# One output projection of batch 1 behind the fourth expert, in place of two parts behind the third and the fourth

## The chip, the cores and the metric

The kernel runs on one core of a Trainium2 chip. The metric is the time of one execution on the device in microseconds (us), lower is better. The engines are named as in the profile: PE (TensorE, the matrix engine), PEld (its weight loads), DVE (VectorE), ACT (ScalarE), POOL (GpSimd) and SP (SyncE, which only issues DMAs here).

## The reference, cut to what matters

Two batches of 512 tokens of width 128 first attend to themselves and to 154 context rows with 16 heads of width 64, and then pass a mixture of eight experts of which each token uses two.

```python
x = x + _L0_xattn_ref(ctx_1024, _layernorm(x), ...)
    # softmax(q k^T / 8) v for 16 heads, out = concat(heads) @ Wout
x = x + _L0_ffn_ref(_layernorm(x), ...)
    # probs = softmax(x @ Wg); the two best of 8, scaled to sum 1
    # out = sum over experts of score * (relu(xm @ W1 + b1) @ W2 + b2)
```

In the kernel the 512 tokens of a batch give the queries, and tokens and context rows together (666) the keys and values.

## The kernel before

The program of each engine is written out by hand, in the order in which it runs; semaphores tie the engines together. An engine that waits holds up everything behind it in its own list.

**Attention.** A step `s` (0 to 15, `STEPS` = 16) handles one pair of heads of one batch; there are `PAIRS` = 8 pairs. `batch_of(s)` and `pair_of(s)` say which: steps 12 to 15 are the pairs 4 to 7 of batch 1. A step makes scores in the PSUM tensor `sc`, ACT takes the exponent, PE multiplies with the values, and ACT copies the unscaled output to `o_t[:, batch, pair, :]` (semaphore `o_copied`). The row sums go from PE through ACT (`copy_sum`, semaphore `sum_copied`) to DVE, which takes four reciprocals of them (L1052, `recip_done`). POOL then multiplies the output by them: `normalise(s)`, L1384, one 128x512 product, which raises `o_norm` by one. `o_norm` at 14 therefore says that pairs 4 and 5 of batch 1 are scaled too, at 16 that pairs 6 and 7 are.

**Output projection.** `out_project(b, bank, pairs)` multiplies, for each of four token tiles of 128 and each pair given, a 128x128 block of `o_t` by a 128x128 block of Wout (L592), and adds all of them up in one PSUM bank. For all eight pairs that is 32 products in the program; the trace has two matmuls for each, 64. For batch 1 the bank is `o_ps`, a half of `xo`. The last matmul of pair 7 raises `out_proj`, on which DVE waits in `x1_and_moments` (L1132).

**Experts.** The loop over `g` (0 to 15) takes eight experts of batch 0 and then eight of batch 1. `layer_one(g)` is six matmuls of 128x512 (L404 to L406, twice), ACT makes relu and a rounded copy of it (L919, L932, L947), POOL and DVE the remainder (`relu_lo`, L1355, L1361, L1190), and `layer_two(g - LAG)` with `LAG` = 2 is six matmuls again (L712, L713, L720). DVE weights an expert's output by the score and adds it up (`add_expert`, L1209 and L1215).

**What hangs on batch 1's projection.** DVE adds the residual (L1132) and takes moments; POOL takes the power (L1412); DVE normalises (L997); PE turns the result (`turn_x2(1)`, L649, behind `layer_one(6)`); DVE splits it; PE makes the gate's logits (L657, behind g = 7); DVE works out the scores; PE turns them (`turn_scores(1)`, L664, behind `layer_one(10)`); ACT copies them (L951); SP writes them to memory and reads them back in eight broadcasts (`spread`, L392). The last three experts scale their hidden values by these (`scale_hidden`, L1201).

**POOL around the change.** In its loop over `g`, POOL works on the remainder of the first half for every `g` (L1355), and between those: for g = 0 `normalise(12)`, `normalise(13)` and a remainder of W2 (L1348); for g = 1 `normalise(14)` and one of W2; for g = 2 two of W2, `normalise(15)`, and three more of W2.

Of the kernel before, what the change touches and what calls it, by code (L numbers as in the profile page):

```python
# [26 lines left out]
PAIRS = H // 2  # L27
STEPS = PAIRS * B
# [57 lines left out]
def xattn_moe(nc, x, ctx_in, g_m, b_m, g_l, b_l, wq, wkv, wout, wg, w1, b1, w2, b2, out):  # L86
    with ExitStack() as stack:
# [6 lines left out]
        def sem(name):  # L94
            return stack.enter_context(nc.semaphore(name))
# [76 lines left out]
        x1_ps = [mx[:, 0, :], o_ps]  # L172
# [78 lines left out]
        o_norm = sem("o_norm")  # L251
# [150 lines left out]
        def _(pe):  # L402
# [104 lines left out]
            def total(s):  # L507
                bank = sum_ps(s)
                if s < HALVED:
                    pe.wait_ge(acc_lo_done, s + 1)  # L510
                    for part in (acc_hi, acc_lo):
                        for h in range(2):
                            mm = pe.matmul(bank[h * HD:(h + 1) * HD, :], ones_h[0:KP, :], part[0:KP, h, :],  # L513
                                           start=(part is acc_hi), stop=(part is acc_lo))
                    mm.then_inc(sum_ready, 1)
                    return
                pe.wait_ge(added, (KT - 1) * (s + 1))
                for h in range(2):
                    mm = pe.matmul(bank[h * HD:(h + 1) * HD, :], ones[0:KP, :], psum_acc[0:KP, s % 2, h, :],
                                   start=True, stop=True)  # L520
                mm.then_inc(sum_ready, 1)
# [67 lines left out]
            def out_project(b, bank, pairs):  # L589
                for t in range(QT):  # L590
                    for r in pairs:
                        mm = pe.matmul(bank[:, t * P:(t + 1) * P], o_t[:, b, r, t * P:(t + 1) * P],  # L592
                                       wout_sb[:, r, :], start=(t == 0 and r == 0),
                                       stop=(t == QT - 1 and r == PAIRS - 1))
                if r == PAIRS - 1:
                    mm.then_inc(out_proj, 1)
# [49 lines left out]
            def turn_x2(b):  # L646
                pe.wait_ge(normed_ready, NORMED0 + QT * (b + 1))
                for t in range(QT):
                    mm = pe.transpose(x2_ps[b][:, t * P:(t + 1) * P], normed[:, b, t, :], ident[:, :])  # L649
                mm.then_inc(x2_turned, 1)  # L650

            def logits(b):
                pe.wait_ge(x2_copied, b + 1)
                if b:
                    pe.wait_ge(x1_ready, 2)
                for t in range(QT):
                    mm = pe.matmul(logits_ps[b][:, t * E:(t + 1) * E], kv_t[:, b, t * P:(t + 1) * P], wg_sb[:, :],  # L657
                                   start=True, stop=True)
                mm.then_inc(logits_ready, 1)

            def turn_scores(b):
                pe.wait_ge(score_ready, b + 1)
                for t in range(QT):
                    mm = pe.transpose(score_ps[b][0:E, t * P:(t + 1) * P], score[:, b, t, :], ident[:, :])  # L664
                mm.then_inc(score_turned, 1)

            def bias_term(b):
                pe.wait_ge(score_copied, b + 1)
                if not b:
                    pe.wait_ge(sum_copied, STEPS - 1)  # L670
                pe.matmul(bias_ps[b], b2_sb[:, :], score_t[:, b, :], start=True, stop=True).then_inc(bias_ready, 1)

            def layer_one(g):
                b, e = g // E, g % E
                if e == 0:
                    pe.wait_ge(x2_lo, b + 1)
                pe.wait_ge(w1_split, min(g + 1, E))
                for c in range(HC):
                    n = g * HC + c
                    if n < 2:  # L680
                        pe.wait_ge(exp_done, STEPS * KT - 1)
                    elif n < 4:
                        pe.wait_ge(sum_copied, STEPS - 1)
                        pe.wait_ge(o_copied, STEPS)
                    elif c == 0:
                        pe.wait_ge(r0_done, g - 1)
                    elif g - 2 in ON_POOL:
                        pe.wait_ge(r1_done, g - 1)
                    else:
                        second_low(pe, g - 2)  # L690
                    three(hid(n), w1_hi[:, e, c * P:(c + 1) * P], w1_lo[:, e, c * P:(c + 1) * P],
                          kv_hi[:, b, 0:N], kv_lo[:, b, 0:N]).then_inc(hid_ready, 1)

            def layer_two(g):
                e = g % E
                if g >= SCALED:
                    if g == SCALED:
                        pe.wait_ge(acc_v, SCALED - 1)
                elif g >= 3:
                    pe.wait_ge(acc_v, g - 2)  # L700
                elif g == 2:
                    pe.wait_ge(bias_copied, 1)
                elif g == 1:
                    pe.wait_ge(score_copied, 1)
                pe.wait_ge(w2_split, min(g + 1, E))
                first, last = g <= SCALED, g < SCALED or g == B * E - 1
                for half, at in enumerate(halves if g >= SCALED else [slice(0, N)]):
                    y = y_ps(g, half)[:, at]
                    for c in range(HC):
                        n = (g * HC + c) % FR  # L710
                        pe.wait_ge(hi1_done if c else hi0_done, g + 1)
                        pe.matmul(y, w2_hi(e)[:, c, :], relu_hi[:, n, at], start=(first and c == 0), stop=False)  # L712
                        pe.matmul(y, w2_lo(e)[:, c, :], relu_hi[:, n, at], start=False, stop=False)  # L713
                    for c in range(HC):
                        n = (g * HC + c) % FR
                        if c:
                            second_low(pe, g)
                        else:
                            pe.wait_ge(lo0_done, g + 1)
                        mm = pe.matmul(y, w2_hi(e)[:, c, :], relu_lo[:, n, at], start=False,  # L720
                                       stop=(last and c == HC - 1))
                    if last:
                        mm.then_inc(y_ready, 1)

            def turn_acc(b):
                pe.wait_ge(acc_v, SCALED if b else E)
                if b:
                    pe.wait_ge(out_ready, 1)
                else:
                    pe.wait_ge(bias_copied, 2)  # L730
                for t in range(QT):
                    mm = pe.transpose(o_ps[:, t * P:(t + 1) * P], acc_t(b)[:, t * P:(t + 1) * P], ident[:, :])
                mm.then_inc(acc_turned, 1)
# [19 lines left out]
            for g in range(B * E):  # L753
                layer_one(g)
                if g == 0:
                    turn_scores(0)
                if g == 1:
                    pe.wait_ge(exp_done, STEPS * KT)
                    total(s)
                if g == 2:  # L760
                    bias_term(0)
                if g == 6:
                    turn_x2(1)
                if g == 10:
                    turn_scores(1)
                if g == 11:
                    bias_term(1)
                if g >= LAG:
                    layer_two(g - LAG)
                if g == 2:  # L770
                    pe.wait_ge(sum_copied, STEPS)
                    pe.wait_ge(o_norm, STEPS - 2)
                    out_project(1, x1_ps[1], range(PAIRS - 2))
                if g == 3:
                    pe.wait_ge(o_norm, STEPS)
                    out_project(1, x1_ps[1], range(PAIRS - 2, PAIRS))
                if g == 7:
                    logits(1)
                if g == 12:
                    turn_acc(0)  # L780
# [681 lines left out]
```

## Time and profile before

| | |
|---|---|
| median of 3 runs | 339.58 us (339.53 to 339.75) |
| the profiled execution | 339.86 us |
| its span, from the first to the last instruction | 338.1 us |
| PE busy | 330.7 us, 98% of the span |
| POOL busy | 293.2 us, 87% |
| DVE busy | 276.4 us, 82% |
| ACT busy | 216.7 us, 64% |
| TensorE clock granted | 1.00 of full speed in all 40 slices |

The profiled execution is the one that the trace shows, and its time lies 1.76 us above its span. It is 0.28 us above the median of the three timed runs. Times in the rows are microseconds from the start of the span. The matmuls are pipelined, so that one listed with 0.39 us may follow the one before it after 0.23 us; the chain of work counts each with what it adds.

### The profile page before, as it was taken

What the parts mean: (1) busy time and instruction counts of PE and PEld (TensorE: products, weight loads), DVE (VectorE), ACT (ScalarE), POOL (GpSimd) and SP (SyncE); (2) the same over time, 40 slices, a digit from 0 to 9 for tenths busy, and PEclk for the clock granted to TensorE, in tenths of its full rate; (3) what the DMA queues carried; (4) which work ended last, traced back from release to release, by engine and by line L of the source; (5) the groups of instructions that cost most, each with busy time, mean ns of one, the idle gap of its engine ahead of it and who ended that gap; (6) DMA issues with size and microseconds to landing.
All of it is one profiled execution on the core that took longest, in us unless ns stands there. A gap on an engine that the chain in (4) does not pass through costs nothing.

```text
span 338.1 us, 6020 instructions
## 1 busy us (share of the span) xinstructions
PE 330.7 (98%) x2209; PEld 220.9 (65%) x2209; DVE 276.4 (82%) x413; ACT 216.7 (64%) x307; POOL 293.2 (87%) x190
## 2 busy tenths in 40 slices
PE   7899999999999999999999999999999999999986
PEld 6676666575747475666657574747585648888766
DVE  5989566988889899999998887989785879489475
ACT  2565678584949484766758585959553746587954
POOL 4549999999999999999999999999996599688763
PEclk9999999999999999999999999999999999999999
DMA  4640000000010100000000000000000006100531
GB/s 128 186 128 0 2 0 4 0 17 0 2 31 3 30 2 0 3 0 3 16 2 16 2 16 17 0 2 0 3 0 3 0 2 211 39 2 0 164 119 34
DMA packets 9050, 10.03 MB, mean 30 GB/s; under 512 B 1015, under 2 KB 6061, under 8 KB 9021
## 3 DMA queue, kind: packets, MB, share of 16 engines
q1 hardware_dynamic: 8725, 9.52, 9.0%
q8 instruction: 18, 0.29, 0.4%
q10 hardware_dynamic: 296, 0.13, 0.1%
q14 instruction: 11, 0.09, 0.1%
HBM read 9.09 MB, written 0.56 MB: 29 GB/s over the span
## 4 chain that ended last, share of the span: by engine, by line
PE 90%; DMA 3%; DVE 3%; ACT 1%; issue 1%; SPq 1%; POOL 0%; DVEq 0%
PE xo L503 23%; PE sc L483 21%; PE sc L489 6%; PE sc L404 5%; PE sc L405 4%; PE sc L406 4%; PE mx L435 3%; PE xo L435 3%; PE mx L592 2%; PE xo L592 2%; PE xo L513 2%; DMA spread<-score_rows 2%; PE sc L503 2%; PE mx L405 1%; PE mx L404 1%; PE mx L406 1%
## 5 line engine op out<-in xcount | busy, mean ns | idle before, releaser
L1377 POOL TENSOR_TENSOR psum_acc<-psum_acc,probs 111x1024 f32<-111x1024 f32 x64 | 164.9, 2576 | 7.0
L816 ACT ACTIVATE probs<-sc 111x1024 f32<-111x1024 f32 x94 | 96.2, 1027 | 17.8 <-PE sc L489 10.5
L483 PE MATMUL sc<-q_pair,k_pair 64*111 64x512 f32 x564 | 83.9, 401 | 0.4 <-ACT v_sb L806 0.4
L503 PE MATMUL xo<-probs,v_sb 111*64 111x512 f32 x360 | 82.7, 596 | 0.0
L483 PEld LDWEIGHTS sc<-q_pair,k_pair 64*111 64x111 f32 x564 | 43.7, 171 | 27.0 <-issue 11.5
L1052 DVE RECIPROCAL recips<-recips 128x128 f32<-128x128 f32 x64 | 54.1, 905 | 0.0
L1018 DVE TENSOR_REDUCE part_max<-mx 128x2 f32<-128x888 f32 x32 | 34.7, 1083 | 20.8 <-PE mx L435 19.3
L503 PEld LDWEIGHTS xo<-probs,v_sb 111*64 111x64 f32 x360 | 24.6, 137 | 38.9 <-issue 35.4
L1377 POOL TENSOR_TENSOR psum_acc<-probs 111x1024 f32<-111x1024 f32 x16 | 39.2, 2453 | 12.3 <-ACT probs L816 12.3
L832 ACT COPY recips<-xo 128x512 f32<-128x512 f32 x15 | 8.8, 586 | 55.2 <-PE xo L513 55.2
L489 PE MATMUL sc<-max_row,ones_r 64*111 64x512 f32 x188 | 37.3, 390 | 0.0
L1018 DVE TENSOR_REDUCE part_max<-xo 128x2 f32<-128x888 f32 x30 | 32.5, 1084 | 1.8 <-PE xo L435 0.3
L1355 POOL TENSOR_TENSOR relu_lo<-relu_ring,relu_hi 128x512 fp32r<-128x512 f32 x16 | 20.7, 1292 | 11.4 <-ACT relu_hi L932 10.0
L1046 DVE TENSOR_TENSOR acc_lo<-psum_acc,acc_hi 111x1024 f16<-111x1024 f32 x15 | 28.6, 1907 | 1.7 <-ACT acc_hi L826 1.7
L1384 POOL TENSOR_TENSOR o_t<-o_t,recips 128x512 f32<-128x512 f32 x16 | 20.7, 1298 | 0.0
L489 PEld LDWEIGHTS sc<-max_row,ones_r 64*111 64x111 f32 x188 | 16.6, 170 | 5.2
L435 PE MATMUL mx<-k_pair,q_pair 64*128 64x444 f32 (+1 forms) x128 | 18.2, 318 | 0.6 <-ACT k_pair L801 0.5
L1022 DVE TENSOR_REDUCE part_max<-mx 128x4 f32<-128x888 f32 x16 | 17.3, 1082 | 1.4
L435 PE MATMUL xo<-k_pair,q_pair 64*128 64x444 f32 (+1 forms) x120 | 17.0, 316 | 0.0
L1022 DVE TENSOR_REDUCE part_max<-xo 128x4 f32<-128x888 f32 x15 | 16.2, 1082 | 0.9
L404 PE MATMUL sc<-kv_hi,wqk_hi 128*128 128x222 f32 (+2 forms) x43 | 16.2, 377 | 0.3 <-ACT v_sb L806 0.3
L826 ACT CAST acc_hi<-psum_acc 111x1024 f16<-111x1024 f32 x15 | 15.8, 1056 | 0.5 <-POOL psum_acc L1377 0.5
(254 smaller groups left out, 622.1 us busy)
## 6 DMA issues: line engine op xcount, KB each, us to landing
spread<-score_rows SPq DMA_DIRECT2D x16, 256.0 KB, 5.5
w_raw<-in_L_ffn_W SPq DMA_DIRECT2D x8, 128.0 KB, 2.1
x_tok<-in_x SPq DMA_DIRECT2D x2, 256.0 KB, 3.1
wv_raw<-in_L_xattn_Wkv SPq DMA_DIRECT2D x4, 128.0 KB, 3.3
wout_sb<-in_L_xattn_Wout SPq DMA_DIRECT2D x1, 512.0 KB
wqk_raw<-in_L_xattn_Wq SPq DMA_DIRECT2D x7, 64.0 KB, 2.0
wqk_raw<-in_L_xattn_Wkv SPq DMA_DIRECT2D x7, 64.0 KB, 2.1
out<-x_tok SPq DMA_DIRECT2D x1, 256.0 KB, 2.0
```

Of the source, the lines that this page charges most:

```text
L404: pe.matmul(out_ap, st_hi, mv_hi, start=True, stop=False)
L435: mm = pe.matmul(to, q_pair[r, n % QKB, 0, t * P:(t + 1) * P], k_pair[r, n % QKB, 0, k_cols(u >= QT)], start=True, stop=True)
L483: pe.matmul(tile_ps(s, kt)[0:KP, h, :], k_pair[r, s % QKB, k_part, at], q_pair[r, s % QKB, q_part, :], start=(k_part + q_part == 0), stop= ...
L489: mm = pe.matmul(tile_ps(s, kt)[0:KP, h, :], ones_r[r, :], max_row[r, s % 2, :], start=False, stop=True)
L503: mm = pe.matmul(out_ps(s)[h * HD:(h + 1) * HD, :], v_sb[0:KP, s // 2 % 2, kt, at:at + HD], probs[0:KP, e % RING, h, :], start=(kt == 0), ...
L816: act.activation(probs[0:KP, e % RING, :, :], tile_ps(s, kt)[0:KP, :, :], ACT.Exp).then_inc(exp_done, 1)
L1018: dve.tensor_reduce(part_max[:, 0, :, u], banks[:, :, 0:KW], AX.X, ALU.max, negate=True) \
L1022: dve.tensor_reduce(part_max[:, 1, :, t:t + 2], banks[:, :, 0:2 * KR].rearrange("p h (t m) -> p h t m", m=KR), AX.X, ALU.max, negate=True) ...
L1046: dve.tensor_tensor(acc_lo[0:KP, :, :], psum_acc[0:KP, s % 2, :, :], acc_hi[0:KP, :, :], ALU.subtract).then_inc(acc_lo_done, 1)
L1052: dve.reciprocal(at, at).then_inc(recip_done, 1)
L1355: pool.tensor_tensor(relu_lo[:, g * HC % FR, :], relu_ring[:, g % 2, :], relu_hi[:, g * HC % FR, :].bitcast(F32), ALU.subtract).then_inc(l ...
L1377: pool.tensor_tensor(psum_acc[0:KP, s % 2, :, :], first, probs[0:KP, e % RING, :, :], ALU.add) \
```

## The change

In the loop over the experts on PE, the part of the projection for pairs 0 to 5 behind `layer_two(0)` is taken out, with its two waits, and the part for pairs 6 and 7 behind `layer_two(1)` becomes one for all eight pairs. Its wait is the sterner of the two, `o_norm` at 16, and the wait for `sum_copied` moves with it. No instruction of another engine changes its place, and the number of products stays at 32 (64 matmuls of the trace).

```diff
                 if g >= LAG:
                     layer_two(g - LAG)
-                if g == 2:
+                if g == 3:
                     pe.wait_ge(sum_copied, STEPS)
-                    pe.wait_ge(o_norm, STEPS - 2)
-                    out_project(1, x1_ps[1], range(PAIRS - 2))
-                if g == 3:
                     pe.wait_ge(o_norm, STEPS)
-                    out_project(1, x1_ps[1], range(PAIRS - 2, PAIRS))
+                    out_project(1, x1_ps[1], range(PAIRS))
                 if g == 7:
                     logits(1)
```

The next two pieces are the difference on PE, in its loop over the experts; a row is an instruction of the program with the tensor that it writes and those that it reads (`sc` holds the hidden values, `mx` and `xo` the outputs). The first place is the end of `layer_two(0)` and the start of `layer_one(3)`:

```order
 L713 MATMUL mx<-relu_hi,w_part 128x512
 L720 MATMUL mx<-relu_lo,wqk_hi 128x512 x2
-L592 MATMUL xo<-wout_sb,o_t 128x128 x24
 L404 MATMUL sc<-kv_hi,w_hi 128x512
 L405 MATMUL sc<-kv_lo,w_hi 128x512
```

The 24 products of pairs 0 to 5 are gone from here, so that `layer_one(3)` follows on `layer_two(0)`. The second place is the end of `layer_two(1)` and the start of `layer_one(4)`:

```order
 L713 MATMUL mx<-relu_hi,w_part 128x512
 L720 MATMUL mx<-relu_lo,wqk_lo 128x512 x2
-L592 MATMUL xo<-wout_sb,o_t 128x128 x8
+L592 MATMUL xo<-wout_sb,o_t 128x128 x32
 L404 MATMUL sc<-kv_hi,w_hi 128x512
 L405 MATMUL sc<-kv_lo,w_hi 128x512
```

All 32 products now stand here, twelve matmuls (`layer_one(3)` and `layer_two(1)`) later than the 24 stood, and in front of `layer_one(4)` as the 8 did.

## Rows read from the trace of the kernel before

**Rows 1.** The page's first part: the span, and each engine's busy time

```profile
span 338.1 us, 6020 instructions
PE 330.7 (98%) x2209; PEld 220.9 (65%) x2209; DVE 276.4 (82%) x413; ACT 216.7 (64%) x307; POOL 293.2 (87%) x190
```

**Rows 2.** PE's waits over the span: us in total, times, longest

```profile
PE sc L525 <- POOL ident L1279: 1.8, 1, 1.8
PE mx L712 <- DVE v_sb L1215: 0.9, 1, 0.9
PE mx L435 <- ACT k_pair L801: 0.5, 1, 0.5
```

**Rows 3.** Busy time by stretch: length, then each engine's busy us

```profile
core 0: us, PE busy (x) PEld busy (x) DVE busy (x) ACT busy (x) POOL busy (x), PEclk, DMA share, GB/s
275.40:292.50 17.10, 17.10 (x104) 13.33 (x103) 10.92 (x15) 11.15 (x19) 17.09 (x16) 1.00 0.38 125
293.20:313.00 19.80, 19.80 (x95) 16.14 (x94) 17.90 (x52) 15.25 (x25) 14.76 (x12) 1.00 0.00 1
```

**Rows 4.** The chain of work around both parts: start, us, what

```profile
283.23 5.36 PE xo L592 x48
288.58 0.24 PE sc L404
...
290.90 0.47 PE mx L720 x2
291.37 1.78 PE xo L592 x16
293.15 0.24 PE sc L404
```

**Rows 5.** POOL's timeline: start, us, line, tensors (idle time before, if any)

```profile
283.37 1.30 POOL L1384 TENSOR_TENSOR o_t<-o_t,recips 128x512 f32<-128x512 f32 x1
...
286.50 0.76 POOL L1348 TENSOR_TENSOR w_part<-w_raw,wqk_lo 128x256 fp32r<-128x256 f32 x1
...
287.87 1.31 POOL L1384 TENSOR_TENSOR o_t<-o_t,recips 128x512 f32<-128x512 f32 x1
289.11 0.76 POOL L1348 TENSOR_TENSOR w_part<-w_raw,wqk_lo 128x256 fp32r<-128x256 f32 x1
```

**Rows 6.** DVE's timeline, from step 15's reciprocals to the normalisation

```profile
282.56 3.37 DVE L1052 RECIPROCAL recips<-recips 128x128 f32<-128x128 f32 x4
...
286.40 0.69 DVE L1209 TENSOR_TENSOR mx<-mx,spread 128x512 f32<-128x512 f32 x1
287.12 0.69 DVE L1215 TENSOR_TENSOR v_sb<-mx,v_sb 128x512 f32<-128x512 f32 x1
291.95 0.69 DVE L1190 TENSOR_TENSOR relu_lo<-sc,relu_hi 128x512 fp32r<-128x512 f32 x1 [4.14 <-ACT relu_hi L947]
...
293.89 0.68 DVE L1132 TENSOR_TENSOR x_tok<-xo,x_tok 128x512 f32<-128x512 f32 x1
...
297.84 1.11 DVE L997 TENSOR_SCALAR normed<-x_tok,moments,rstd 128x128 f32<-128x128 f32 x4 [0.54 <-POOL rstd L1412]
```

**Rows 7.** What `layer_two(1)` reads: ACT's, DVE's and POOL's last parts

```profile
280.31 0.58 ACT L947 CAST relu_hi<-sc 128x512 fp32r<-128x512 f32 x1
282.02 0.63 DVE L1190 TENSOR_TENSOR relu_lo<-sc,relu_hi 128x512 fp32r<-128x512 f32 x1
282.12 1.31 POOL L1355 TENSOR_TENSOR relu_lo<-relu_ring,relu_hi 128x512 fp32r<-128x512 f32 x1
```

**Rows 8.** The chain at PE's late wait, where it starts anew

```profile
328.86 0.70 DVE v_sb L1215
329.60 0.38 PE mx L712
329.99 0.12 PE mx L713
```

**Rows 9.** The matmuls of L592 alone: min, median, max ns

```profile
L592 PE MATMUL xo<-wout_sb,o_t x64: 271/275/275, 283.1 to 292.9; 128*128 128x128 f32 x64
```

**Rows 10.** The chain at `turn_scores(1)` and the broadcasts behind it

```profile
312.60 0.45 PE xo L664 x4
...
313.07 0.59 ACT psum_acc L951
...
313.68 1.44 DMA score_rows<-psum_acc
...
317.40 6.06 DMA spread<-score_rows
```

## The prediction

> **What bounds the kernel now.** I read the page's first part, then PE's waits, then the stretch around the two parts of the projection, then the chain of work up to the end. PE is busy 330.7 of 338.1 us [rows 1], and its three largest waits are 1.8, 0.9 and 0.5 us [rows 2], the first two of them at the very start and near the very end. The stretch that holds the change and all that follows it up to the turned scores has none: PE is busy 17.10 of 17.10 us from 275.40 to 292.50, and 19.80 of 19.80 from 293.20 to 313.00 [rows 3]. So in this stretch the end of PE's list sets the time, and each microsecond that PE stands still there moves everything on PE behind it. The second engine to watch is POOL: it too is busy 17.09 of 17.10 us in the first of these stretches [rows 3]. Its list has no slack there, so what it releases comes at the times that the rows show, and no earlier.
>
> From 313 us on the chain leaves PE: it runs from the turned scores (312.60) through ACT's copy (313.07), the write to memory (313.68) and the last broadcast that matters (from 317.40, 6.06 us) [rows 10]. The chain's first link is a PE instruction behind the change, so a delay of PE moves this chain by as much. That is why I don't look for slack in the end, though PE has its 0.9 us of waiting there [rows 2].
>
> **What is removed and added.** The matmuls are the same 64. In two parts they take 5.36 and 1.78 us of the chain [rows 4], together 7.14 us, or 0.1116 us each in both parts. In one part they take 7.14 us too. Nothing of the work goes away, so the sum is about one thing only, when PE can start them.
>
> **When PE comes to them.** PE reaches the place of the first part at 283.23. Now layer_one(3) and layer_two(1) follow there. In the trace of before these two take from 288.58 to 291.37 [rows 4], 2.79 us. Moved forward they need to find their inputs ready at 283.23 and some 1.4 us later. For layer_two(1) these are ACT's rounded copy (280.31 and 0.58, so 280.89), DVE's remainder (282.65) and POOL's (282.12 and 1.31, so 283.43) [rows 7]. Halfway through the two groups PE is at 284.6, so the latest of the three is there 1.2 us before it is wanted. layer_one(3) reads weights and tokens that the earlier experts have used already, and overwrites banks whose readers are the same copy and remainder, finished by 282.65. So PE passes both without a wait and stands before the projection at 283.23 + 2.79 = 286.02.
>
> **What it finds there.** The one part waits for o_norm at 16, the last scaled pair. POOL starts that product at 287.87 and takes 1.31 us [rows 5], so it ends at 289.18. Before, the first part asked only for pair 5, two POOL products earlier in the list (the product of pair 6 is the one at 283.37 [rows 5]), and the part that asks for pair 7 came at 291.37, 2.19 us after it was ready. Now PE is early by 289.18 - 286.02 = 3.16 us. Could the product come sooner? Its other input, step 15's reciprocals, is done at 282.56 + 3.37 = 285.93 [rows 6], but POOL is in the middle of its list then and has no idle time to give up [rows 3]. POOL's list is not changed.
>
> **What the wait costs beside its length.** A release takes a moment, and PE starts empty behind it. The only late wait of PE shows both: DVE ends at 328.86 + 0.70 = 329.56, PE begins at 329.60, and its first matmul adds 0.38 us where the next add 0.12 [rows 8]. For the release I take 0.04. For the first matmul I take as the lower end the matmul's own length of 0.275 us [rows 9] less the 0.11 that it adds when pipelined, 0.16, and as the upper end the 0.26 of that late wait, which has the loading of the weights in it. The wait thus costs 3.16 + 0.04 + 0.16 to 0.26 = 3.36 to 3.46 us, and I take 3.4. This stands on the end of a POOL span, and the page says that these are rough: POOL's next operation begins at 289.11 [rows 5], which would make it 0.07 less.
>
> **What it gives back.** Nothing that I can find. PE does layer_one(3) 5.36 us earlier, so ACT works on it in what was idle time, and DVE's L1190 for it (before at 291.95, after 4.14 us of idling) and the two additions behind it move to about 288 [rows 6]. But from 293.20 to 313.00 PE waited for no engine [rows 3], so inputs that come earlier shorten nothing there. The projection ends at 293.15 + 3.4 = 296.55. Before, the residual (L1132) began at 293.89, 0.74 us after the projection, since DVE was adding an expert; now DVE is free and begins at once. This 0.74 us is not on the path: POOL's power for the norm stands behind the remainder of layer_one(4), which moves by 3.4 us with PE, and PE turns the normed tokens by its own order, behind layer_one(6). The norm ends at 297.84 + 1.11 = 298.95 [rows 6], before PE gets there at about 300; with both moved by 3.3 to 3.4 us this margin stays. The gate's scores, their turn and the broadcasts move by 3.4 us as one piece.
>
> **The sum.** Against the profiled execution, 339.86 + 3.4 = 343.26. That execution is 0.28 above the median of the timed runs, so the median of the changed kernel should be near 343.0, 1.0% more. A difference of 0.2%, 0.7 us, is about what can be told from no change in this kernel.
>
> **Rivals.**
>
> *The clock falls behind the wait (9 in 100).* In all rows of this trace the granted clock is 1.00 [rows 3], the upper level of 2.4 GHz, and PE's longest wait is 1.8 us [rows 2]; it has never stood still for 3.2 us. A fall to 1.2 GHz would double what a PE-bound matmul takes. Its price is between nothing and the whole projection at half speed, 7.14 us more; in between I take 1.7 us, a slow stretch as long as the wait of 3.4 us, half of which is lost: 343.0 + 1.7 = 344.7, and at the upper end 350.1. It decides if the clock reacts to this wait at all. Against it stands only that the 1.8 us did nothing. The Trainium skill (TensorE: Matmul & The Clock Gate, "HAM oscillation — how this bites in real kernels") describes kernels that fall to the lower clock in each of their waits for a transfer, of a few microseconds. By it this wait is at the edge; no run so far shows which side.
>
> *The end takes part of it up (6 in 100).* If the last broadcasts were held by something other than the turned scores, PE's late wait of 0.94 us could shrink first: 343.0 - 0.9 = 342.1. Against it: the chain goes through the scores, with gaps of 0.02 us between them and the copy [rows 10].
>
> *POOL's last product comes later than before (3 in 100).* DVE's remainder and additions for experts 3 and 1, 3 x 0.69 = 2.1 us, now run beside it. If they hold up POOL, the wait grows by at most that: up to 345.1. Against it: POOL's W2 remainder takes 0.76 us at 286.50, beside DVE's additions, and 0.76 at 289.11, beside an idle DVE [rows 5, 6].
>
> *Not slower (4 in 100).* If pair 7 is scaled before PE stands there, the wait is not there, and the time is 339.6. This needs the last POOL product to end by 286.02, 3.2 us before its row says. It could come so only if POOL's list ran otherwise than its rows; the reciprocals, done at 285.93, would leave the product no time even then. So it would take a misread wait: that PE isn't held by this product at all. The mechanism gives no gain, since no work goes away.
>
> **How the numbers follow.** The forecast, a full wait with nothing given back, has 78 in 100 and gives 342.6 to 343.6: the bounds of the start cost and of POOL's end, and 0.3 us for a median of few runs. The range runs from 342.4 to 344.6: below it lie the part given back and the case without a wait (10 in 100), above it most of the falling clock (some 6). Of the cases, only the misread wait gives no change or, by chance, a gain: faster 0.01, same 0.03, slower 0.96.
>
> **What the new profile would show.** A wait of PE at L592 for POOL's L1384, of 3 us or more, the only large one of PE, from about 286.1 to 289.2; 64 matmuls behind it in 7.1 to 7.4 us; L1384's last product still at about 287.9; layer_one(4) at about 296.6 in place of 293.15; DVE's L1132 at once behind the projection; turned scores at about 316.0 in place of 312.60; the granted clock 1.00. The prediction is wrong if PE waits for less than 2.9 us, if layer_two(1) waits for a remainder, if the turned scores come later by less than the wait, or if matmuls behind the wait take twice 0.11 us.

## The result and the profile after

The changed kernel takes 345.73 us in the median of 6 executions (344.89 to 346.25), against 339.64 us (339.25 to 339.77) for the kernel before beside it: 1.0168 times the time, with a 95% interval of 1.0153 to 1.0183. It is slower, as forecast, but by 6.1 us between the medians (5.7 by the ratio) and not by 3.4, and the time lies above the range. The profiled execution is the fastest of the six, 344.89 us, 5.03 above the profiled one of before (339.86).

PE's waits in the changed kernel, us in total, times, longest; they answer to [rows 2]:

```profile
PE xo L592 <- POOL o_t L1381: 3.4, 1, 3.4
PE sc L525 <- POOL ident L1276: 1.8, 1, 1.8
PE mx L712 <- DVE v_sb L1212: 0.8, 1, 0.8
```

The wait that was forecast is there, for the product foretold and of about the length foretold, and it is the only new one. (Lines from L777 on stand three lower than before: L1381 is L1384 of before.) PE's timeline at the place, and POOL's at its last product, which answer to [rows 4] and [rows 5]:

```profile
283.01 0.40 PE L404 MATMUL sc<-kv_hi,w_hi 128*128 128x512 f32 x1
...
285.32 0.63 PE L720 MATMUL mx<-relu_lo,wqk_lo 128*128 128x512 f32 x2
289.31 9.01 PE L592 MATMUL xo<-wout_sb,o_t 128*128 128x128 f32 x64 [3.36 <-POOL o_t L1381]
298.08 0.48 PE L404 MATMUL sc<-kv_hi,w_hi 128*128 128x512 f32 x1
```

```profile
287.89 1.28 POOL L1381 TENSOR_TENSOR o_t<-o_t,recips 128x512 f32<-128x512 f32 x1
```

PE passes layer_one(3) and layer_two(1) with no wait, stands still for 3.36 us, and starts the 64 matmuls at 289.31, when POOL's product has ended at 289.17. But from there to layer_one(4) it takes 8.77 us and not 7.14. The reason is in the stretches, with the granted clock as the third number from the end:

```profile
core 0: us, PE busy (x) PEld busy (x) DVE busy (x) ACT busy (x) POOL busy (x), PEclk, DMA share, GB/s
286.00:289.60 3.60, 0.29 (x2) 0.32 (x3) 3.53 (x6) 1.02 (x2) 3.60 (x5) 1.00 0.52 193
289.60:293.00 3.40, 3.40 (x19) 3.40 (x18) 0.07 (x1) 0.00 (x0) 2.85 (x4) 0.50 0.00 0
293.00:298.00 5.00, 5.00 (x46) 5.00 (x46) 0.00 (x0) 0.00 (x0) 0.00 (x0) 1.00 0.00 0
```

For 3.4 us TensorE runs at 0.50, the level of 1.2 GHz (the slow stretch, in what follows). It has 19 matmuls in these 3.4 us, and 46 in the 5.0 us behind them. The fall came about 0.3 us after PE had begun to work again, not in the wait. DVE stood at the residual all the time:

```profile
298.36 0.69 DVE L1129 TENSOR_TENSOR x_tok<-xo,x_tok 128x512 f32<-128x512 f32 x1 [8.69 <-PE xo L592]
...
302.87 1.12 DVE L994 TENSOR_SCALAR normed<-x_tok,moments,rstd 128x128 f32<-128x128 f32 x4 [0.48 <-POOL rstd L1409]
```

The chain's rows that answer to [rows 10] stand 5.14 us later, and the last broadcast takes 0.13 us less:

```profile
317.74 0.45 PE xo L664 x4
...
318.22 0.59 ACT psum_acc L948
...
318.82 1.44 DMA score_rows<-psum_acc
...
322.54 5.93 DMA spread<-score_rows
```

The profiled execution's 5.0 us of span (343.1 against 338.1) can thus be added up. The wait: PE would have started at 283.01 + 2.86 = 285.87 (2.86 us from one L404 to the place, as before from 288.34 to 291.20 in PE's timeline); it started at 289.31, 3.44 later, and started empty, 0.15 more (the 64 matmuls take 7.14 us behind a wait at full clock, as e1_filled shows, and took 6.99 in two parts in the same view of before). The clock: 8.77 - 7.14 = 1.63. Together 5.22, less 0.05 for coming to the place earlier, which is the 5.17 by which layer_one(4) moved (292.91 to 298.08). The rows of PE's timeline of before that this uses:

```profile
283.06 5.52 PE L592 MATMUL xo<-wout_sb,o_t 128*128 128x128 f32 x48
288.34 0.48 PE L404 MATMUL sc<-kv_hi,w_hi 128*128 128x512 f32 x1
...
291.20 1.95 PE L592 MATMUL xo<-wout_sb,o_t 128*128 128x128 f32 x16
292.91 0.48 PE L404 MATMUL sc<-kv_hi,w_hi 128*128 128x512 f32 x1
```

### The profile page after: what moved, and what is told of

Read it like the earlier page. It is cut to its first block, busy times and chain, and to the rows that moved or that the text cites. A ratio compares the mean times of both kernels' runs of the same rounds, so it can differ in the third digit from the quotient of the medians.

```text
span 343.1 us, 6020 instructions
## 1 busy us (share of the span) xinstructions
PE 332.4 (97%) x2209; PEld 223.0 (65%) x2209; DVE 275.6 (80%) x413; ACT 216.7 (63%) x307; POOL 293.2 (85%) x190
## 4 chain that ended last, share of the span: by engine, by line
PE 85%; POOL 7%; DVE 2%; DMA 2%; issue 2%; ACT 1%; SPq 1%; POOLq 0%; DVEq 0%
PE xo L503 23%; PE sc L483 20%; PE sc L489 6%; PE sc L404 4%; PE sc L405 3%; PE sc L406 3%; POOL psum_acc L1374 3%; PE mx L435 3%; PE xo L435 3%; PE xo L592 3%; PE mx L592 2%; PE xo L513 2%; DMA spread<-score_rows 2%; PE mx L405 1%; PE mx L404 1%
## 5 line engine op out<-in xcount | busy, mean ns | idle before, releaser
L1381 POOL TENSOR_TENSOR o_t<-o_t,recips 128x512 f32<-128x512 f32 x16 | 20.7, 1294 | 0.0
L916 ACT ACTIVATE relu_ring<-sc,cols 128x512 f32<-128x512 f32 x13 | 8.9, 688 | 14.2 <-PE sc L406 13.0
L404 PE MATMUL sc<-kv_hi,wqk_hi 128*128 128x222 f32 (+2 forms) x43 | 16.2, 378 | 0.3 <-ACT v_sb L803 0.3
```

The lines of the kernel that those rows point to most:

```text
L404: pe.matmul(out_ap, st_hi, mv_hi, start=True, stop=False)
```

## The experiments

Each edit is shown against the changed kernel. Line numbers below an edit shift by a few. What a group of matmuls costs on PE's path is the time from its start to the start of the next instruction; the second number of its row is larger, since the last matmul's own length is in it (the projection's row of 7.38 us in e1_filled is 7.14 us on the path).

**e1_filled: the wait without the standing still.**

```diff
                 if g == 3:
+                    pe.wait_ge(bias_copied, 1)
+                    for _ in range(14):
+                        pe.matmul(pj[:, 0:P], ident[:, :], ident[:, :], start=True, stop=True)
                     pe.wait_ge(sum_copied, STEPS)
                     pe.wait_ge(o_norm, STEPS)
```

> The changed kernel, with 14 products of the identity with itself (28 matmuls of 128 columns, about 3.1 us) that PE does in the wait, into a bank that is free, and whose result nobody reads. Theory (the wait alone costs 3.4 us, and the rest, 2.7 us of the median, comes from TensorE's clock, which falls because PE stands still): the clock is granted at 1.00 throughout, the projection's 64 matmuls take 7.1 us again in place of 9.0, POOL's last product is no earlier, and the time is 342.9 to 343.3, the one that was forecast. Rival (the 64 matmuls are slow since they stand in one group or beside POOL's work, whatever the clock did before): they take 9.0 us again and the time stays at 345 to 346.

The wait for `bias_copied` makes sure that the bank `pj` has been read before the added products write to it.

Measured: 343.81 us in the median of 5 (342.55 to 344.16) against 340.00 for the kernel before beside it, a ratio of 1.0102 (1.0087 to 1.0118). The profiled execution took 343.36. PE's timeline and the stretches:

```profile
285.66 3.29 PE L773 MATMUL xo<-ident 128*128 128x128 f32 x28
289.19 7.38 PE L592 MATMUL xo<-wout_sb,o_t 128*128 128x128 f32 x64 [0.25 <-POOL o_t L1384]
296.33 0.47 PE L404 MATMUL sc<-kv_hi,w_hi 128*128 128x512 f32 x1
```

```profile
286.00:289.20 3.20, 2.95 (x28) 2.79 (x26) 3.13 (x6) 0.89 (x2) 3.20 (x5) 1.00 0.64 243
289.20:296.30 7.10, 7.10 (x63) 7.10 (x64) 0.34 (x1) 0.00 (x0) 3.12 (x4) 1.00 0.00 0
```

The same group at the same place, started within 0.12 us of the same moment and beside the same work of POOL, takes 7.14 us when PE has been busy before it. The clock stays at 1.00, and the pace agrees: 64 matmuls in 7.1 us. The rival is out: the slow matmuls are the clock's, and the clock falls because of the standing still. What is left, 1.0% or 3.5 us by the ratio, is the wait as forecast. The median of 343.81 is 0.5 us over the expectation, but that was made from a before of 339.6, and before took 340.00 here.

**e2_two_waits: the place without the wait.**

```diff
                     pe.wait_ge(sum_copied, STEPS)
+                    pe.wait_ge(o_norm, STEPS - 2)
+                    out_project(1, x1_ps[1], range(PAIRS - 2))
                     pe.wait_ge(o_norm, STEPS)
-                    out_project(1, x1_ps[1], range(PAIRS))
+                    out_project(1, x1_ps[1], range(PAIRS - 2, PAIRS))
```

> The changed kernel with all 32 products at the new place behind the fourth expert, but in two groups: pairs 0 to 5 behind the wait for 14 scaled pairs, then pairs 6 and 7 behind the wait for 16. Theory (only the sterner wait in front of products that were ready costs anything): PE comes to the first group at 286.0 and finds its pairs scaled, and to the second at 291.4, 2.2 us after the last pair is scaled, so it waits for neither: 339.5 to 339.8, no change from before. Rival (the place itself costs, since DVE stands at the residual earlier in its list and the work behind it is late): PE waits behind the projection, and the time is 0.5 us or more above before.

Measured: 340.19 us in the median of 12 (339.24 to 341.11) against 340.00, a ratio of 1.0002 (0.9990 to 1.0014). No change that can be told; the interval leaves room for at most 0.5 us. PE's timeline has the 64 matmuls with no wait in front:

```profile
285.99 7.31 PE L592 MATMUL xo<-wout_sb,o_t 128*128 128x128 f32 x64
293.05 0.48 PE L404 MATMUL sc<-kv_hi,w_hi 128*128 128x512 f32 x1
```

So neither the place nor DVE's longer standing at the residual costs anything. The whole loss comes from asking for the last pair before any product is made.

**e3_pool_sooner: a shorter wait.**

```diff
                 if g == 2:
-                    w2_low(3)
-                    w2_low(4)
                     normalise(STEPS - 1)
-                    for e in range(5, E):
+                    for e in range(3, E):
                         w2_low(e)
```

> The changed kernel with POOL's last product moved ahead of two remainders of W2 (2 x 0.7 us), so that it ends at 287.8 in place of 289.2. PE waits 1.8 to 1.9 us in place of 3.4. Theory (the clock falls behind a long wait only; the 1.8 us at the very start did nothing): the clock stays at 1.00, the projection takes 7.1 us, and the time is 339.6 + 1.9 + 0.2 = 341.7. Rival (the clock falls behind each wait of about 2 us in this place too): the projection takes 8 to 9 us, and the time is 343.5 to 344.5.

Measured: 342.69 us in the median of 5 (342.26 to 343.30) against 340.00, a ratio of 1.0078 (1.0066 to 1.0091), or 2.65 us. The wait, the projection and what follows:

```profile
288.93 7.38 PE L592 MATMUL xo<-wout_sb,o_t 128*128 128x128 f32 x64 [2.00 <-POOL o_t L1381]
296.07 0.48 PE L404 MATMUL sc<-kv_hi,w_hi 128*128 128x512 f32 x1
```

A wait of 2.0 us leaves the clock at 1.00 and the projection at 7.14 us. The time is 2.9 us under the changed kernel beside it, of which 1.4 are the shorter wait. By the ratio it stands 0.5 us above my 2.1 (interval 2.2 to 3.1). The wait itself is as expected, 2.00 us with its release. The profiled execution, the slowest of the five (343.30), shows where its own time went: PE came to the place 0.9 us later than in the first profile of the changed kernel, a delay that arose at the start of the span (see e10_again2). How much of it the median has is not shown.

**e4_again: the changed kernel, unchanged.**

> The changed kernel once more, unchanged, for a second profile. Six executions of it gave 344.89 to 346.25, a spread of 1.4 us where before has 0.5. Theory (the slow stretch begins at different moments against the wait, so that it has a different length in each execution): another profile shows a wait of the same 3.4 us and a projection of another length than 9.0 us, longer by about what its time is above 344.9. Rival (the wait differs): the wait is longer or shorter than 3.3 to 3.5 us and the projection is again 9.0.

Measured: 345.62 us in the median of 5 (344.75 to 347.64) against 340.00, a ratio of 1.0173 (1.0150 to 1.0196), which repeats the first result. Its profile is of its fastest execution, 344.75 us, and shows a wait of 3.35 us, a projection of 8.94 us, and the clock at the lower level from 288.9 to 292.3, again for 3.4 us but 0.7 us sooner:

```profile
288.90:292.30 3.40, 3.24 (x15) 3.27 (x16) 0.54 (x1) 0.00 (x0) 3.30 (x5) 0.50 0.00 0
```

The slow stretch thus does begin at another moment in another execution. But neither expectation is met: the wait and the projection are both about the same as in the first profile. Since the time was the same as in the first profile too, the profile told nothing of the spread. The mean granted clock that is on record for each execution does tell something. It is 0.995 in the three profiles of the changed kernel, each with 3.4 us at 0.50 (half of 3.4 us lost in 343 is 0.005). Of the first result's six executions five have 0.995 and the highest, 346.25, has 0.990; of the five of this run, four have 0.995 and the highest, 347.64, has 0.990. By this measure a slow stretch of twice the length belongs to the highest execution of each set, and the medians (345.73, 345.62) are of executions with the short one.

**e5_half_filled, e6_fill3 and e9_fill5: how long PE may stand still.** The edit is e1_filled's with 7, 3 and 5 products in place of 14, so that PE stands still for 1.8, 2.7 and 2.2 us at the end of the wait. The product that it waits for comes as late in all of them.

> As e1_filled, but with 7 products (14 matmuls, 1.6 us) that PE does first in the wait, so that it stands still for the last 1.8 us of it. Theory (a wait of under 2 us lets the clock be, as in e3_pool_sooner): granted clock 1.00, projection 7.1 us, and the same time as e1_filled, 1.0% above before, 3.4 to 3.6 us. Rival (any standing still just ahead of the projection costs clock): projection over 7.5 us, time between those of e1_filled and of the changed kernel, 4.2 us or more above before.

> As e1_filled, but with 3 products (6 matmuls, 0.7 us), so that PE stands still for the last 2.7 us. This lies between the waits seen so far: 2.0 us let the clock be, 3.35 us did not. Theory (the clock falls if PE's rest happens to be long enough where the chip looks, so that it is a matter of the execution in between): executions of both kinds, a median between 3.5 and 5.5 us above before and a spread of 1.5 us or more. Rival (a sharp bound above 2.7 us): as e1_filled, 3.4 to 3.6 us above before. Rival (a sharp bound below it): as the changed kernel, 5.5 to 6 us.

> As e1_filled, with 5 products (10 matmuls, 1.1 us), so that PE stands still for the last 2.2 us of the wait. 2.0 us (e3_pool_sooner) and 1.8 us (e5_half_filled) let the clock be, 2.7 us (e6_fill3) did not. If 2.2 us is short enough too, 3.4 to 3.8 us above before and a clock of 1.00; if the bound lies between 2.0 and 2.2 us, 5 to 6 us above; executions of both kinds would give something between with a spread of 1.5 us or more.

| kernel | standing still | median (lowest to highest) | against before (95% interval) |
|---|---|---|---|
| e1_filled | 0.25 us | 343.81 (342.55 to 344.16) | 1.0102 (1.0087 to 1.0118) |
| e5_half_filled | 1.80 us | 343.59 (343.36 to 343.86) | 1.0101 (1.0086 to 1.0116) |
| e9_fill5 | 2.24 us | 345.12 (342.65 to 346.42) | 1.0137 (1.0093 to 1.0180) |
| e6_fill3 | 2.70 us | 345.40 (344.88 to 345.79) | 1.0153 (1.0135 to 1.0170) |
| e4_again | 3.35 us | 345.62 (344.75 to 347.64) | 1.0173 (1.0150 to 1.0196) |

1.8 us costs nothing beyond the wait (the mean clock of 0.998 in its profile comes from the last 1.1 us of the span, when PE has done its work). 2.7 us costs nearly what the whole 3.4 us do, in each of five executions (the fifth is e11_fill3_again below), two of them profiled. So the sharp bound below 2.7 us comes nearest; the spread of 1.5 us or more that my theory asked for isn't there (0.9 us). Between them, 2.24 us gave executions of both kinds: 342.65 and 343.33 with a mean clock of 0.999 and 1.000, and four from 345.00 to 346.42 with 0.995; the profiled one, 343.33, has a clock of 1.00 and a projection of 7.38 us. The clock does not react to a wait of a set length alone; the same program falls or doesn't. e6_fill3's profile showed something else that no theory of mine had, a projection of 10.33 us:

```profile
289.27 10.33 PE L592 MATMUL xo<-wout_sb,o_t 128*128 128x128 f32 x64 [2.70 <-POOL o_t L1384]
299.35 0.47 PE L404 MATMUL sc<-kv_hi,w_hi 128*128 128x512 f32 x1
```

```profile
286.00:288.60 2.60, 0.57 (x6) 0.38 (x4) 2.56 (x5) 0.98 (x2) 2.60 (x4) 1.00 0.93 325
288.60:295.30 6.70, 6.03 (x28) 6.06 (x29) 1.00 (x2) 0.00 (x0) 3.80 (x5) 0.50 0.02 6
295.30:299.00 3.70, 3.70 (x35) 3.70 (x34) 0.00 (x0) 0.00 (x0) 0.00 (x0) 0.98 0.00 0
```

Here the clock fell 0.7 us before PE went to work, which is 2.0 us after PE had stopped, and stayed down for 6.8 us (the 0.98 of the next stretch holds the last 0.1 of them), twice the other length. It costs 10.08 - 7.14 = 2.94 us. The other three executions of e6_fill3 have a mean clock of 0.995, so the short length, against 0.989 here.

**e11_fill3_again: the same kernel, for a second profile.**

> e6_fill3 once more, for a second profile. Theory (the slow stretch's length hangs on when it begins against the end of the wait, so that it can be 3.4 or 6.7 us in the same kernel): a time of 344.0 to 344.4 with a projection of 8.9 to 9.1 us, or of 345.5 to 345.9 with one of 10.3 us. Rival (its length is fixed by the kernel): 10.3 us again, and 345.5 to 345.9.

Measured: one execution, 345.02 us, with the same wait and a projection of 9.01 us:

```profile
289.41 9.01 PE L592 MATMUL xo<-wout_sb,o_t 128*128 128x128 f32 x64 [2.69 <-POOL o_t L1384]
```

```profile
289.40:290.00 0.60, 0.59 (x5) 0.60 (x6) 0.38 (x1) 0.00 (x0) 0.60 (x2) 1.00 0.06 24
290.00:293.30 3.30, 3.30 (x18) 3.30 (x18) 0.00 (x0) 0.00 (x0) 2.55 (x3) 0.52 0.00 2
```

This time the clock fell 0.7 us after PE had begun, and was low for the short length. The length is not fixed by the kernel, as the theory had it; the time of 345.02 is between the two bands that I had written down.

**e7_longer and e8_longer_filled: a wait of 6.1 us.** The first moves the one part to g = 2, the second fills the wait there with 27 products.

```diff
-                if g == 3:
+                if g == 2:
                     pe.wait_ge(sum_copied, STEPS)
                     pe.wait_ge(o_norm, STEPS)
                     out_project(1, x1_ps[1], range(PAIRS))
```

> The changed kernel with the whole projection one expert sooner, behind the third expert's first layer and the first one's second. PE comes to it at 283.2 and waits for the same POOL product, 6.1 us. Theory (the clock falls once in a wait, and comes back some 3.5 us after PE works again, however long the wait was): the projection takes 8.9 to 9.1 us as in the changed kernel, and the time is 6.3 us for the wait and 1.9 to 2.7 us for the clock, 8.2 to 9.0 us above before. Rival (the longer PE rests the longer its clock stays low): the projection takes over 10 us, and the time is 10 us or more above before.

> As e7_longer, with 27 products of the identity (54 matmuls, 6.0 us) that PE does in the wait. Theory (the clock's part can be taken away in the longer wait too): clock 1.00, projection 7.1 us, time 6.2 to 6.5 us above before, 1.9 to 2.7 less than e7_longer. Rival (the dummies, or their bank, cost something themselves that e1_filled hid): more than 6.8 us above before.

Measured: e7_longer 348.54 us in the median of 5 (347.84 to 348.74), 1.0238 (1.0221 to 1.0254) of before's 340.11; e8_longer_filled 346.74 us in the median of 4 (346.10 to 347.47), 1.0194 (1.0174 to 1.0213). e7_longer at the place:

```profile
289.52 9.38 PE L592 MATMUL xo<-wout_sb,o_t 128*128 128x128 f32 x64 [6.06 <-POOL o_t L1381]
```

```profile
282.00:286.60 4.60, 1.46 (x6) 0.84 (x5) 4.60 (x7) 2.85 (x5) 4.60 (x5) 1.00 0.83 292
286.88:293.70 6.82, 4.18 (x19) 4.21 (x20) 1.12 (x2) 0.00 (x0) 4.55 (x6) 0.50 0.21 79
```

The clock was low for 6.8 us (and all five executions have a mean clock of 0.990, as such a length gives), but 2.6 of them lay in the wait, where they cost nothing, so that the projection took 9.38 us, 0.4 more than in the changed kernel and above the 8.9 to 9.1 that I expected: the clock came back 4.2 us after PE worked again (293.70 - 289.52), not 3.5. e8_longer_filled had a clock of 1.00 and a projection of 7.38 us. The clock's part in the longer wait is 1.8 us by the medians, just under the 1.9 expected, and the wait's own part is 1.94% or 6.6 us, just above the 6.5. The rival of a projection over 10 us is out. The rival that the added products cost something is not out by the time alone, since the interval reaches 7.2 us; against it stands the profile, with the projection as long as in e1_filled and a time of 346.10 us, 6.2 above the profiled execution of before.

**e10_again2: the changed kernel a third time.**

> The changed kernel a third time, for one more profile. Theory (the slow stretch has one of two lengths, 3.4 us as in the two profiles of this kernel, or 6.7 us as in the profiles with waits of 2.7 and 6.1 us, and the median of the timed runs, 345.7, has executions of both in it): an execution of 344.7 to 345.1 has 3.4 us of slow clock and a projection of 8.9 to 9.0 us; one of 346 or more has over 3.4 us of it and a projection of 9.5 us or more. Rival (what differs between executions lies elsewhere): an execution of 345.5 or more with a projection of 9.0 us.

Measured: one execution of 346.37 us, and the rival is right about it: the wait (3.36) and the projection (9.01 us) are those of the first profile, though the time is 1.5 us more.

```profile
290.21 9.01 PE L592 MATMUL xo<-wout_sb,o_t 128*128 128x128 f32 x64 [3.36 <-POOL o_t L1381]
```

```profile
318.67 0.45 PE xo L664 x4
...
319.74 1.45 DMA score_rows<-psum_acc
...
323.53 6.44 DMA spread<-score_rows
```

PE came to the place 0.9 us later (its wait began at 286.85 against 285.95), and the last broadcast took 6.44 us in place of 5.93. Both are in parts that the change leaves alone. The late coming is there in full at the start of the span, where the first matmul of 512 columns begins at 12.65 us in this profile, at 12.79 in e3_pool_sooner's and at 11.69 in the changed kernel's first:

```profile
12.06 0.47 PE L435 MATMUL mx<-k_pair,q_pair 64*128 64x444 f32 x2 [0.54 <-ACT k_pair L798]
...
12.65 0.50 PE L404 MATMUL xo<-kv_hi,wqk_hi 128*128 128x512 f32 x1
```

In both of the later ones DVE also waited for the load of the context (0.3 and 0.4 us), which it doesn't in the first. What makes the start later in some executions is not shown.

## Why the prediction was right and where it failed

**Right.** PE has no wait between 283 us and its turned scores (317.74) other than the new one, so nothing of the delay was hidden, and nothing was given back: layer_one(4) moved by 5.17 us and the turned scores by 5.14. layer_one(3) and layer_two(1) found their inputs ready. POOL's last product ended at 289.17, forecast 289.18, untouched by DVE's work that now lies beside it. The norm ended at 303.99, and PE turned it at about 305, with the margin of 1 us that it had. e2_two_waits shows that the place is free.

**The size of the wait** was forecast as 3.36 to 3.46 us with its start, and was 3.44 + 0.15 = 3.59 in the profile. Two terms were off. The release was taken as 0.04 us from a wait for DVE; from the end of POOL's span to PE's start it was 0.14. And PE's coming, 286.02, was worked out from the chain's rows but POOL's end from the timeline: in PE's timeline every place is 0.17 us earlier than in the chain (283.06 against 283.23), and PE would have started at 285.87. The runs with the clock at 1.00 agree with it: 1.02% or 3.5 us in e1_filled, 3.4 in e5_half_filled.

**The step that failed** is the term that the sum put at nothing, the clock: the projection was to take 7.14 us at a granted clock of 1.00, and took 8.77 us, with 3.4 us at 0.50. The rival "the clock falls behind the wait", to which I gave 9 in 100, is what happened in all three profiles of the changed kernel. The prediction's own sign, matmuls behind the wait at twice 0.11 us, was met while the clock was low, since 1.63 of the 3.4 us were lost. I argued against it from PE's 1.8 us at the start of the span, which "did nothing". That row was misread. These are the first matmuls behind that wait in the kernel before, and the same matmuls a little later:

```profile
1.84 3.77 PE L525 MATMUL sc<-ident 128*128 128x128 f32 x16 [1.84 <-POOL ident L1279]
5.54 0.23 PE L545 MATMUL xo<-ident,rows 20*128 20x20 f32 x1
...
7.57 0.83 PE L525 MATMUL sc<-ident 128*128 128x128 f32 x6
```

```profile
2.00:4.00 2.00, 2.00 (x10) 2.00 (x11) 0.40 (x2) 0.96 (x1) 0.62 (x4) 1.00 0.75 244
```

They need nothing but `ident`, and PE is busy throughout. The first 16 take (5.54 - 1.84) / 16 = 0.23 us each, and 28 like them in e1_filled 3.29 / 28 = 0.12, half as much. So PE began at the lower level, though the profile gives 1.00 for this stretch (third number from the end), and a wait there could not bring the clock down. The longest wait of before that lay in a stretch at full clock is the 0.9 us near the end, 2.4 us under the new one, and the trace held no evidence on waits of 3 us. The experiments gave it: 1.8 and 2.0 us let the clock be, 2.24 us didn't always, and 2.7 us made it fall each time. The Trainium skill (TensorE: Matmul & The Clock Gate, "HAM oscillation — how this bites in real kernels") told of a kernel that falls in each of its waits of some 3 to 5 us, as this one does at 3.36, and should have had more weight than that row.

**Its price** was taken as 1.7 us, and is 1.63 in the first profile, 2.94 in the worse of the two kinds that e6_fill3 shows, and 1.8 by the medians of e4_again and e1_filled (2.4 by their ratios, 1.0173 and 1.0102). With it the forecast for this case was 344.7 for the median, and 345.0 for the profiled execution, which took 344.89. That it came so near is in part luck: it took the slow stretch to be as long as the wait, and behind the wait of 2.7 us it was 3.4 us in one execution and 6.8 in another. So the last 1.0 us to the median of 345.73 is not in the profile that was taken: I had put the median 0.28 us below the profiled execution, as before, and it came out 0.84 above. The longer slow stretch is not the reason, since five of the six executions have the mean clock of 0.995 that goes with the short one; it may be behind the highest alone (346.25, with 0.990), though no profile of the changed kernel has caught it. An execution with a later start and a slower broadcast (e10_again2: 0.9 and 0.5 us) would do it, but why the changed kernel's executions should have these more often than those of before, whose six lie within 0.5 us, stays open.

## What to carry to other kernels

A wait moved in front of work that was ready costs its full length where the engine has no other wait behind it, and on TensorE it may cost more than its length. Before adding one, look for the longest wait in the trace that lay in a stretch at full clock and left it there, and check the clock by the pace of equal matmuls too, since a row at the start can say 1.00 and be slow. That wait is a lower bound on what is safe in most executions. Above it nothing is known. The price is half of the part of the slow stretch in which PE works. If the wait can't be avoided, products that nobody reads, done in it, buy the clock back (1.8 us here), but waiting per part, so that the ready products go first, buys everything back.

## What the runs showed of the hardware that was not expected

Three matters. First, TensorE's clock went down for 3.4 us in four profiles (three of the changed kernel, one of e6_fill3's kernel) and for 6.8 us in two, always to 0.50. The short ones began between 0.2 us before and 0.7 us after PE went to work again, the long ones 0.7 us (e6_fill3) and 2.6 us (e7_longer) before it. A fall could thus come when PE was already working again. Second, the same program with a standing still of 2.24 us took 342.65 or 346.42 us: near such a bound the time of a kernel is not one number, and few executions can mislead. Third, the kernel before isn't quite free of it: of its 37 executions beside the experiments, 36 took 339.48 to 340.92 us at a mean clock of 0.998 or more, and one took 343.22 at 0.995. It has no profile, so what stood still in it is not known.
